# One wait for all scores of a tile, in place of one for each pair of heads

## The reference, cut to what matters

```python
xq = _ada_ln(x_q, t_vec, Wss_q, bss_q)
xkv = _ada_ln(x_kv, t_vec, Wss_kv, bss_kv)
q = (xq @ Wq + bq).reshape(B, Lq, nh, dh)
kv = (xkv @ Wkv + bkv).reshape(B, Lkv, 2, nh, dh)
k = kv[:, :, 0]
v = kv[:, :, 1]
scores = jnp.einsum('bqhd,bkhd->bhqk', q, k) / jnp.sqrt(jnp.float32(dh))
attn = jax.nn.softmax(scores, axis=-1)
out = jnp.einsum('bhqk,bkhd->bqhd', attn, v).reshape(B, Lq, H)
return x_q + (out @ Wp + bp)
```

## Time and profile before

| | us |
|---|---|
| time, median of 3 runs | 2184.37 (2181.47 to 2184.44) |
| time of the profiled execution | 2181.79 |
| its span | 2179.6 |
| PE busy | 2153.8 (99%) |
| DVE busy | 1913.6 (88%) |
| ACT busy | 1817.8 (83%) |

### The profile page before, as it was taken

The page is one execution under the profiler, slowest core; times in us unless marked ns, Lnnn a source line. Parts: engine busy times, 40 slices in busy tenths (PEclk is TensorE's granted clock), DMA queues, the critical chain, the costliest instruction groups (busy, mean ns, idle before and its releaser), DMA issues.

```text
span 2179.6 us, 56041 instructions
## 1 busy us (share of the span) xinstructions
PE 2153.8 (99%) x24986; PEld 622.7 (29%) x24986; DVE 1913.6 (88%) x1179; ACT 1817.8 (83%) x1908; POOL 17.3 (1%) x28
## 2 busy tenths in 40 slices
PE   7999999999999999999999999999999999999998
PEld 3444322222222222222222222222222222222222
DVE  2435798899999899999999999999999999989998
ACT  1221899999999999999999999999999999998995
POOL 0001000000000000000000000000000000000000
PEclk9999999999999999999999999999999999999999
DMA  8345522234222422233223322233223322242221
GB/s 297 142 165 181 162 73 56 75 93 115 71 80 77 130 69 77 65 98 109 81 70 99 107 82 69 77 96 106 69 81 89 99 74 77 70 115 83 77 54 51
DMA packets 189011, 210.23 MB, mean 96 GB/s; under 512 B 17238, under 2 KB 120414, under 8 KB 188764
## 3 DMA queue, kind: packets, MB, share of 16 engines
q1 hardware_dynamic: 187180, 206.06, 32.4%
q10 hardware_dynamic: 1584, 0.53, 0.1%
HBM read 169.33 MB, written 37.22 MB: 95 GB/s over the span
## 4 chain that ended last, share of the span: by engine, by line
PE 96%; DVE 1%; issue 1%; ACT 1%; DMA 0%; POOL 0%; SPq 0%; ACTq 0%; DVEq 0%
PE bank L1091 40%; PE bank L1103 36%; PE bank L1120 4%; PE bank L1171 4%; PE bank L1009 4%; PE bank L1020 4%; PE bank L1133 1%; PE bank L1146 1%; PE bank L1229 1%; PE bank L989 1%; ACT arena L1340 1%; DVE stats L1440 0%; DVE arena L1648 0%; PE bank L1156 0%; DVE arena L1454 0%
## 5 line engine op out<-in xcount | busy, mean ns | idle before, releaser
L1340 ACT ACTIVATE arena<-bank,shift 128x1024 f32<-128x1024 f32 x1600 | 1692.4, 1115 | 156.8 <-PE bank L1091 145.6
L1648 DVE TENSOR_TENSOR arena<-arena 128x2048 f32<-128x2048 f32 x736 | 1656.5, 2287 | 113.4 <-ACT arena L1340 105.0
L1091 PE MATMUL bank<-qs,ks 32*64 32x512 f32 x12800 | 938.3, 613 | 1.1 <-ACT arena L1301 0.7
L1103 PE MATMUL bank<-arena,vg 128*32 128x512 f32 x6400 | 852.3, 605 | 1.1 <-ACT arena L1340 1.1
L1091 PEld LDWEIGHTS bank<-qs,ks 32*64 32x64 f32 x12800 | 216.1, 129 | 380.4 <-issue 197.2
L1103 PEld LDWEIGHTS bank<-arena,vg 128*32 128x32 f32 x6400 | 125.9, 108 | 650.4 <-ACT arena L1340 649.6
L1171 PE MATMUL bank<-wp,arena 128*32 128x168 f32 (+2 forms) x2464 | 153.6, 321 | 0.0
L1120 PE MATMUL bank<-xt,wq 128*32 128x256 f32 x1792 | 137.7, 379 | 0.0
L1171 PEld LDWEIGHTS bank<-wp,arena 128*32 128x32 f32 x2464 | 80.0, 110 | 184.4 <-issue 163.9
L1301 ACT ACTIVATE arena<-bank,bk_c 128x512 f32<-128x512 f32 (+1 forms) x28 | 18.0, 642 | 129.9 <-PE bank L1009 129.9
L1120 PEld LDWEIGHTS bank<-xt,wq 128*32 128x32 f32 x1792 | 58.2, 110 | 134.1 <-issue 118.1
(11 more groups left out here) (88 smaller groups left out, 418.9 us busy)
## 6 DMA issues: line engine op xcount, KB each, us to landing
ks<-k_full SPq DMA_DIRECT2D x160, 320.0 KB, 3.1
vg<-v_full SPq DMA_DIRECT2D x160, 320.0 KB, 3.9
p_b<-p_tails SPq DMA_DIRECT2D x128, 128.0 KB, 4.1
arena<-in_x_dram SPq DMA_DIRECT2D x13, 1024.0 KB, 8.1
q_full<-qs SPq DMA_DIRECT2D x32, 256.0 KB, 2.0
out_dram<-arena SPq DMA_DIRECT2D x32, 256.0 KB, 2.0
arena<-l_recip SPq DMA_DIRECT2D x28, 256.0 KB, 5.6
arena<-in_ctx_dram SPq DMA_DIRECT2D x6, 1024.0 KB, 13.5
```

The lines of the kernel that those rows point to most:

```text
L1091: mm = nc.tensor.matmul(bank[out, 2 * (i % RING) + h % 2, :], ks[rows_of(h), keys], qs[rows_of(h), g, :], start=True, stop=True)
L1103: mm = nc.tensor.matmul(bank[rows_of(h), o_bank(u), :], vg[:, t, rows_of(h)], pt[t % PR][:, h, :], start=(t == 0), stop=False, skip_group_ ...
L1340: nc.scalar.activation(pt[t % PR][:, 2 * pair:2 * pair + 2, :], bank[:, first:first + 2, :], ACT.Exp, scale=SCALE, bias=shift[:, g:g + 1]) ...
L1648: nc.vector.tensor_tensor(a[:, :, :], (pt[t - 1] if k <= 2 else a)[:, :, :], pt[t % PR][:, :, :], ALU.add).then_inc(p_added, 1)
```

## The change

The number of instructions and their order is the same on every engine. What differs is which matmul carries the wait for `e_done`. Before, each pair waited for its own slot. Now the first matmul of a tile waits for the slot of the second pair (`n + 1`), and the second pair has no wait.

```diff
                         for pair in range(2):
                             i = n + pair
-                            if i >= RING:
-                                pe.wait_ge(e_done, i - RING + 1)
+                            if pair == 0 and n + 1 >= RING:
+                                pe.wait_ge(e_done, n + 1 - RING + 1)
                             for side in range(2):
```

## The result

| | before | changed |
|---|---|---|
| median of 4 runs | 2184.01 us | 2231.24 us (2229.86 to 2232.10) |
| profiled execution | 2181.79 | 2230.53 |
| its span | 2179.6 | 2228.8 |

The ratio is 1.0222, 95% interval [1.0209, 1.0235]: 2.2% slower, 47 us. Forecast was slower by 36.4 us, 2219.5 us in a range of 2203 to 2233.

The account below looks back on a forecast made before the run. Hand-overs between PE and ACT, not PE's 99% busy share, were taken to bound it. Interval terms of 37.4 us less 1.0 at the end gave +36.4; forecast 2219.5 us, own range 2206 to 2231, stated range 2203 to 2233.

Parts of the forecast that it names:

- The ring of two tiles: PE and ACT loop in tiles without side job: first exponential, second pair, weighing, first pair, exponential; 4.42 us for two tiles.
- narrow tiles: 252 tiles with a narrow output job: weigh intervals of 2.33 us rise by 0.07, of 2.37 by 0.025.
- intervals under 2.40 are lifted, others stay: Between weigh groups: no tile follows another in under 2.40 us; 370 intervals rise to that, longer ones stay.
- Wide tiles: 378 tiles with 256-column side jobs, transposes or sums: scores 2.47 us apart, wait already met, no loss.
- free tiles: 170 tiles without a side job: weigh intervals of 2.04 us rise by 0.36, of 2.38 by 0.025.
- I take zero: Removing the wait between a tile's two pairs of score matmuls gains nothing; bounds 0 and 0.03 us a tile.
- hand-over of 0.06: From the end of a tile's first exponential on ACT to the scores it releases on PE: 0.06 us.
- the end: Last tiles: DVE catches up, so PE no longer waits 0.96 us for it; gives back 1.0 us, bounds 0 and 1.0.
- the rival of the clock: Pauses of 0.3 us in free tiles drop PE's clock to 1.2 GHz: about 2500 us, chance 0.02.
- No change: Rival: PE is 99% busy and the early first pair only spares ACT waiting where it has slack: 2184 us, chance 0.06.
- Faster: Rival: PE occupation bounds, so joining pairs saves up to 0.34 us in about 85 split tiles: 2155 us, chance 0.03.
- half of it: Rival: exponential follows in under 1.24 us and narrow tiles stay as they are: about +15 us, 2199 us, chance 0.06.

Follow-up runs that it names:

- Experiment 2: Changed kernel with the two waits of every fifth tile swapped and the single wait only in even-numbered tiles, per-pair waits elsewhere: 2189.72 us, ratio 1.0033 to the kernel before.
- experiment 1: Changed kernel with the two waits of every fifth tile's first score matmul swapped, e_done first, then keys: 2222.33 us, ratio 1.0182 to the kernel before.
- experiment 3: Changed kernel with swapped fifth-tile waits and the single wait only in the 378 wide tiles, per-pair waits elsewhere: ratio 1.0005 to the kernel before.
- experiment 4: Changed kernel with swapped fifth-tile waits and the single wait only in the 252 narrow tiles, per-pair waits elsewhere: ratio 1.0067 to the kernel before.
- experiment 6: Kernel before without the first pair's wait for its own slot, the second pair keeping its wait: 2181.95 us, ratio 0.9999 to the kernel before.
- experiments 7: Changed kernel with an extra, already met wait ahead of e_done in every tile without a keys wait: 2259.03 us, ratio 1.0350 to the kernel before.

## Why the prediction was right, and where it fell short

**Direction and mechanism: right.** The ring of two tiles, E0 - second pair - weighing - first pair - E0, was turned into one of a single tile, and 2.40 us was read from the trace before as 4.42 less 1.02 and 1.00; the timeline after has 2.40 and 2.41. Experiment 2 shows the ring itself: with every second early pair left in place 82% of the loss is gone. One reading of the ring was wrong and changed nothing: in the narrow tiles it doesn't hold the 0.29 of side job "twice". 4.70 is 4.42 and 0.28, one side job; the second one of the two tiles does not lie on the way from E0 to E0.

**The rule "intervals under 2.40 are lifted, others stay": right.** 370 intervals were under 2.39 before; in experiment 1's trace 4 are. Wide tiles are unchanged in experiment 3. In the changed kernel itself they are not quite: "if the 2.47 tiles grow" was a sign of being wrong, and 49 of them, each a fifth tile, went from 2.47 to 2.50. The reason is the step below, and not the ring.

**The classes.** By the forecast's own list free tiles are 26.2 (8.1 + 3.9 + 18 x 0.41 + 0.2 + 0.8 + 3 x 1.95), narrow ones 11.2 (18 x 0.54 + 3 x 0.5) and wide ones nothing. The expectations for the experiments split the same 37.4 into 27 and 10.5. In the trace of experiment 1 the intervals that hold the scores of free tiles grew by 27.2, of narrow ones by 12.3, of wide ones by 0.3. So each term of the ring was right to about 1 us; the 14.6 of the narrow tiles alone has an interval of 11.6 to 17.7 and holds 1.3 that arise only where this class stands alone (two intervals of 0.03 in each unit, experiment 4).

**The wait taken away from between the pairs, "I take zero": not contradicted.** Experiment 3 takes it away in 378 tiles, where it had been met, at 1.1 us (-0.9 to 3.1). Where it was not met it can't be taken away apart from the ring. The first pair's own wait, "empty" in the forecast, was worth nothing (experiment 6).

**The step that failed.** The sentence "It adds and removes no instruction, on no engine and in no DMA queue" hid it. That is true of the count, yet each fifth tile has an extra semaphore instruction, and by the change the late condition landed on it. I had taken the hand-over of 0.06 as one number for all tiles. In the 151 intervals ahead of such a tile in which an excess shows (102 of about 0.09, 49 of about 0.03), the trace after is over the forecast's rule by 11.1 us. The same sum is 1.1 in the trace of experiment 1, of which 1.0 are the tiles with a third wait. So the term is worth 10 us in the traces and 8.6 by the run times (48.4 less 39.8), and it makes up most of the 11 to 13 us that the forecast lacked. That the total fell into the range all the same is in part luck: 2231.24 lies just outside the forecast's own 2206 to 2231, which was made for errors of the ring, and 1.8 us inside the stated range.

**The sum.** Over the intervals between weigh groups the changed kernel lost 49.7 us: 37.8 by lifting all to 2.403, 11.1 by the fifth tiles, 0.8 elsewhere. The first weigh group came 0.6 later (the last one 50.3 later, 2205.68 against 2155.36 in the earlier trace rows), and the end gave back 1.1 (forecast 1.0). The span grew by 49.2.

**What should show.** Free tiles don't alternate any more, but every fifth interval is 2.49. No groups of 8 loads: right. PE's share 97%: it is 96%. ACT's wait about 180: 197.1. L1241 without a wait: right. Clock 1.00, in the stretch view of the changed kernel:

```profile
28.00:2210.00 2182.00, 2114.64 (x24878) 586.45 (x24877) 1903.37 (x1132) 1816.24 (x1900) 14.21 (x16) 1.00 0.32 92
```

So 170 pauses of 0.3 us did not bring the granted clock down from its 2.4 GHz level, and the rival of the clock falls. With it falls, for this kernel, the swing that the Trainium skill describes for short idle times ("TensorE: Matmul & The Clock Gate", A second HAM failure mode: psum-queue depth-cycling). "No change" (busy PE, waits are free) is refuted by the time and by the 170 waits of PE. "Faster" is refuted too: the group with the common start still reaches the weighing only 1.05 after it (274.62, 275.67), and it starts 0.06 after the end of E0, as the second pair did before. The "half of it" case, +15 us, lies far below the interval.

**Left open.** Why the loads of a group released through the extra instruction take 0.27 and not 0.24 was not tried; of its 0.09 us, 0.06 are the later start and 0.03 these loads. No version faster than the kernel before came out: the experiments remove waits that were already met, and the shortest ring found is its own.

## What to carry to other kernels

If the second of two groups has to wait, holding the first until the same moment is not free, although the second loses nothing. Look for what the early group starts on another engine, and follow that chain through all engines until it closes on itself. The time of one pass divided by the tiles that it spans is what a tile costs; an engine that is 99% busy can still be driven by such a ring. Where an instruction has two waits, write the one that comes last so that the instruction itself carries it, and let the met one go to the extra semaphore instruction.

## What the runs showed of the hardware that was not expected

A late condition on the separate semaphore instruction in PE's queue (51 ns) costs about 0.08 to 0.09 us more than the same condition on the weight load itself, in tiles that are held by it (median interval 2.485 against 2.404 in experiments 7 and 1). A met condition there costs nothing that could be measured, some 640 times over (ratio 1.0184 against 1.0182). In these kernels the wait that was written second in the program went to the separate instruction.
